# A fused Mamba-like block and FP4 feed-forward on one core: the gate and silu(z) moved within a step, h's transposes kept together, and a down product of 17 passes

## What is computed

```
x_proj, z = split(x @ W_in)                      # 512 + 512 columns
x_conv = silu(causal_conv4(x_proj) + conv_b)
ssm = x_conv @ W_xproj                           # 1 + 16 + 16 columns
delta = softplus(ssm[..., 0]);  B, C = ssm[..., 1:17], ssm[..., 17:]
h_mean = einsum("bld,bln->bdn", x_conv, delta * B) / L     # over the whole sequence
y = (einsum("bdn,bln->bld", h_mean, C) + D * x_conv) * silu(z)
x1 = layernorm(x + y @ W_out)
h = silu(q(x1) @ q(w_gate).T) * (q(x1) @ q(w_up).T)        # 704 columns
out = layernorm(x1 + q(h) @ q(w_down).T)
```

## Time and profile before

| | us |
|---|---|
| median of 3 runs (2201.85 to 2204.41) | 2202.8 |
| the profiled execution | 2204.03 |
| its span, first to last instruction | 2202.1 |
| PE busy | 1990.6 (90%) |
| DVE busy | 1756.7 (80%) |
| POOL busy | 1115.6 (51%) |
| ACT busy | 1111.5 (50%) |

### The profile page before, as it was taken

The page is one execution under the profiler, slowest core; times in us unless marked ns, Lnnn a source line. Parts: engine busy times, 40 slices in busy tenths (PEclk is TensorE's granted clock), DMA queues, the critical chain, the costliest instruction groups (busy, mean ns, idle before and its releaser), DMA issues.

```text
span 2202.1 us, 37847 instructions
## 1 busy us (share of the span) xinstructions
PE 1990.6 (90%) x10532; PEld 1583.8 (72%) x10532; DVE 1756.7 (80%) x3548; ACT 1111.5 (50%) x2100; POOL 1115.6 (51%) x1643
## 2 busy tenths in 40 slices
PE   1887899899999999899999999899999999877776
PEld 1655688688877888688877888688876888666665
DVE  6234788798978888789877888798887888788875
ACT  2665455555545555455544556455544555423332
POOL 2223455466545556455644555465554556445543
PEclk9999999999999999999999999999999999999998
DMA  2111111111111111111111111111111111000000
GB/s 79 50 56 43 34 49 44 44 43 45 49 41 34 44 48 45 36 49 49 41 38 41 44 44 48 38 49 44 39 41 39 49 45 35 29 20 25 20 20 15
DMA packets 77089, 90.53 MB, mean 41 GB/s; under 512 B 8881, under 2 KB 59953, under 8 KB 76849
## 3 DMA queue, kind: packets, MB, share of 16 engines
q1 hardware_dynamic: 76848, 87.73, 12.2%
HBM read 37.37 MB, written 16.78 MB: 25 GB/s over the span
## 4 chain that ended last, share of the span: by engine, by line
PE 76%; issue 5%; DVE 4%; ACT 3%; POOL 1%; ACTq 0%; DVEq 0%; POOLq 0%
PE pgu L489 23%; PE pd L489 14%; PE pd L537 9%; PE pa L489 6%; PE pb L489 6%; PE pc L571 4%; PE pc L519 4%; PE pe_ L631 2%; PE pa L559 2%; PE pc L496 2%; PE pe_ L548 1%; PE pd L638 1%; DVE hbuf L990 1%; DVE qsh L820 1%; PE pa L615 1%
## 5 line engine op out<-in xcount | busy, mean ns | idle before, releaser
L489 PE MATMUL pgu<-wgu_hi,xqT 128*128 128x512 f32 (+1 forms) x1536 | 427.7, 387 | 0.9 <-issue 0.9
L489 PE MATMUL pd<-wd_hi,hqT 128*128 128x256 f32 (+1 forms) x1536 | 334.5, 299 | 18.7 <-DVE r L1012 15.5
L489 PEld LDWEIGHTS pgu<-wgu_hi,xqT 128*128 128x128 f32 x1536 | 279.8, 190 | 75.8 <-issue 27.6
L537 PE MATMUL pd<-wout,g 128*128 128x256 f32 x1024 | 259.9, 398 | 49.6 <-DVE hqT L980 35.2
L489 PEld LDWEIGHTS pd<-wd_hi,hqT 128*128 128x128 f32 (+1 forms) x1536 | 255.8, 190 | 57.4 <-issue 23.8
L946 DVE SCALAR_TENSOR_TENSOR acc<-xps,cw,acc 128x512 f32<-128x512 f32 x256 | 248.7, 972 | 24.4 <-POOL acc L429 23.7
L418 POOL TENSOR_SCALAR rs<-mv 128x1 f32<-128x1 f32 x128 | 61.6, 481 | 396.4 <-DVE mv L1027 228.8
L537 PEld LDWEIGHTS pd<-wout,g 128*128 128x128 f32 x1024 | 191.5, 195 | 79.7 <-issue 56.0
L741 ACT ACTIVATE hqT<-pe_ 128x512 fp32r<-128x512 f32 x128 | 76.2, 595 | 335.3 <-PE pe_ L631 335.3
L402 POOL TENSOR_TENSOR xv<-xnq,qsx 128x256 f32<-128x256 bf16 x128 | 79.5, 621 | 300.1 <-DVE xnq L839 300.1
L489 PE MATMUL pgu<-wgu_lo,xqT 128*128 128x512 f32 (+1 forms) x768 | 228.3, 379 | 0.0
(11 more groups left out here) (132 smaller groups left out, 4669.2 us busy)
## 6 DMA issues: line engine op xcount, KB each, us to landing
xcr<-xcs SPq DMA_DIRECT2D x128, 256.0 KB, 2.3
xin<-in_L_attn_x_dram SPq DMA_DIRECT2D x32, 512.0 KB, 3.9
xres<-in_L_attn_x_dram SPq DMA_DIRECT2D x128, 128.0 KB, 2.1
out_dram<-outb SPq DMA_DIRECT2D x128, 128.0 KB, 1.7
szr<-in_L_attn_W_in_dram SPq DMA_DIRECT2D x1, 1024.0 KB, 7.4
szr<-in_L_ffn_w_down_dram SPq DMA_DIRECT2D x1, 704.0 KB, 8.6
szr<-in_L_ffn_w_gate_dram SPq DMA_DIRECT2D x1, 640.0 KB, 4.5
szr<-in_L_ffn_w_up_dram SPq DMA_DIRECT2D x1, 640.0 KB, 5.7
```

The lines of the kernel that those rows point to most:

```text
L489: mm = pe.matmul(bank, lhsT, rhs, start=(m == 0), stop=(m == len(pairs) - 1))
L537: mm = pe.matmul(pd[:, 0:DM], g[:, (s + 1) % 2, c, j * P:(j + 1) * P], wout[:, c, :], start=(c == 0), stop=(c == NB - 1))
```

## The change

Four edits, all in the steps and in the weights' setup.

1. The last chunk of h (64 columns) is written twice by POOL, side by side, in place of 64 columns of zeros, and the last chunk of the down weights is laid out twice: in wd_hi, rows 0 to 63 keep the high half, and rows 64 to 127 hold the low half. One pass over 128 rows then gives high x high and high x low, and one over 64 rows low x high: 17 passes in place of 18.
2. The banks pd and pe_ become one tensor pde of two banks. The six transposes of h go to its last 768 columns with one semaphore increment, and ACT and DVE each take them in one instruction. They have waited for r1 and r2 from the first transpose on.
3. POOL's gate stands behind the history copy and xprod.
4. ACT's silu(z) stands behind the first tap and the copy of the transposed x.

```diff
@@ POOL, setup
+            pool.wait_ge(wq_ready, 3)
+            for h in range(KM):
+                rest = quant_w[2][:, h * FF + FC * P:(h + 1) * FF]
+                pool.tensor_copy(twice_d[:, h * P:h * P + FR], rest)
+                last = pool.tensor_copy(twice_d[:, h * P + FR:(h + 1) * P], rest)
+            last.then_inc(wq_ready, 1)
@@ POOL, body
-                    if p2 and not late_y(j, s):
-                        gate(i, j, s, w)
                     if p1:
...
                         pool.tensor_tensor(blocks(xv[:, :]), blocks(xnq[:, :]), spread(qsx[:, 1, :]),
                                            ALU.mult).then_inc(xprod_done, 1)
+                    if p2 and not late_y(j, s):
+                        gate(i, j, s, w)
...
                         pool.wait_ge(hq_link, 6 * tg + 6)
+                        at_least(pool, hq_pe, tg)
+                        pool.tensor_tensor(blocks(hbuf[:, 2 * FF:FF + (FC + 1) * P]), blocks(hnq[:, FC * P:FF]),
+                                           spread(qsh[:, 1, FC * P // QB:QH]), ALU.mult)
                         pool.tensor_tensor(blocks(hbuf[:, FF:2 * FF]), blocks(hnq[:, :]),
                                            spread(qsh[:, 1, :]), ALU.mult).then_inc(hprod_done, 1)
@@ PE
-                for c in range(FC + 1):
-                    m_ = P if c < FC else FR
-                    pairs += [(hqT[0:m_, c, :], wd_hi[0:m_, c, :]),
-                              (hqT[0:m_, c, :], wd_lo[0:m_, c, :]),
-                              (hqT[0:m_, FC + 1 + c, :], wd_hi[0:m_, c, :])]
-                split_product(pd[:, 0:DM], DM, pairs).then_inc(dn_pe, 1)
+                for c in range(FC):
+                    pairs += [(hqT[:, c, :], wd_hi[:, c, :]),
+                              (hqT[:, c, :], wd_lo[:, c, :]),
+                              (hqT[:, FC + 1 + c, :], wd_hi[:, c, :])]
+
+                pairs += [(hqT[:, FC, :], wd_hi[:, FC, :]),
+                          (hqT[0:FR, 2 * FC + 1, :], wd_hi[0:FR, FC, :])]
+                split_product(pde[:, 0:DM], DM, pairs).then_inc(dn_pe, 1)
...
-                        for n in range(4):
-                            mm = pe.transpose(pe_[:, n * P:(n + 1) * P],
-                                              hbuf[:, FF + n * P:FF + (n + 1) * P], ident[:, :])
-                        mm.then_inc(hq_pe, 1)
-
                         at_least(pe, r_done, capped(to, NT))
                         at_least(pe, r2_done, td)
-                        for n in range(4, FC + 1):
-                            mm = pe.transpose(pd[:, (n - 4) * P:(n - 3) * P],
-                                              hbuf[:, FF + n * P:FF + (n + 1) * P], ident[:, :])
+                        for n in range(FC + 1):
+                            mm = pe.transpose(hq_cols[:, n * P:(n + 1) * P], hbuf[:, FF + n * P:FF + (n + 1) * P],
+                                              ident[:, :])
                         mm.then_inc(hq_pe, 1)
@@ ACT
-                    if not late_y(j, s) and p1:
-                        silu_z(i, j, s, u, w)
...
                         act.activation(xqT[:, 0:KM, :], pe_[:, 0:DM].rearrange("p (c n) -> p c n", c=KM), ACT.Copy)\
                             .then_inc(xqT_hi, 1)
+                    if not late_y(j, s) and p1:
+                        silu_z(i, j, s, u, w)
@@ DVE, weights
                 dve.wait_ge(wt_hi, n + 1)
+                if lo is None:
+                    dve.tensor_tensor(hi[FR:P, :], (pa, pb)[n % 2][FR:P, 0:DM], hi[FR:P, :], ALU.subtract)\
+                        .then_inc(wt_lo, 1)
+                    continue
```

More of the change, by code:

```diff
@@ L460, in weight_groups @@
                         groups.append((P, pieces, wgu_hi[:, k, lo:lo + width], wgu_lo[:, k, lo:lo + width]))
-            for c in range(FC + 1):
-                m = P if c < FC else FR
-                pieces = [(quant_w[2][:, h * FF + c * P:h * FF + c * P + m], P) for h in range(KM)]
-                groups.append((m, pieces, wd_hi[0:m, c, :], wd_lo[0:m, c, :]))
+            for c in range(FC):
+                pieces = [(quant_w[2][:, h * FF + c * P:h * FF + (c + 1) * P], P) for h in range(KM)]
+                groups.append((P, pieces, wd_hi[:, c, :], wd_lo[:, c, :]))
+            pieces = [(twice_d[:, h * P:(h + 1) * P], P) for h in range(KM)]
+            groups.append((P, pieces, wd_hi[:, FC, :], None))
             return groups
         W_GROUPS = weight_groups()
-        W_NEEDS = [1] * 4 + [2] * 4 + [3] * (FC + 1)
+        W_NEEDS = [1] * 4 + [2] * 4 + [3] * FC + [4]
         @block.tensor
@@ L1011, in body @@
                         dve.wait_ge(xres_landed[j % 2], 16 * (2 * i + j // 2 - 1))
-                        dve.tensor_tensor(r1[:, j, :], pd[:, 0:DM], xres[:, j % 2, :], ALU.add)\
+                        dve.tensor_tensor(r1[:, j, :], pde[:, 0:DM], xres[:, j % 2, :], ALU.add)\
                             .then_inc(r_done, 1)
@@ L1040, in body @@
                         at_least(dve, out_ready, td)
-                        dve.tensor_tensor(r2[:, :], pd[:, 0:DM], r1[:, (j - 3) % TPS, :], ALU.add)\
+                        dve.tensor_tensor(r2[:, :], pde[:, 0:DM], r1[:, (j - 3) % TPS, :], ALU.add)\
                             .then_inc(r2_done, 1)
```

47 lines of the change are left out of this document (21 added, 26 removed).

## The result

The changed kernel takes 2221.2 us (median of four runs, 2221.0 to 2223.4) against 2202.3 for the kernel before: 1.0087 times, with a 95% interval of 1.0069 to 1.0104. The direction is the one forecast, but the forecast was 2240 us, +37, and the loss is 18.9, half of that.

A forecast was written before the change was run, and what follows sets the result against it. PE, tied with a loop through ACT, DVE and POOL, bounds the middle; a chain bounds the tail. Middle +14.3, +4.2, +6.6, passages +3.6, tail +13.2, start -5: +37, 2240 us; range 2228 to 2253, 8 in 10 2213 to 2257.

The forecast's parts named there:

- The tail: Steps after the last input supertile, bound by a chain: +0.94 us in each of 14 with a gate, +13.2.
- the caught scale: DVE's 44-column scale of h, blocked until POOL's running gate ends: +0.90 us in the tail, partly absorbed in middle steps.
- the row: h's transposes in one 768-column row: covered in the middle, +0.16 us on the tail's x chain.
- The step from j = 2: Middle step to j = 3, bound by the h transposes' loop: +0.55 us in each of 26 steps, +14.3.
- The second write: POOL's 64-column write ahead of hprod, in the loop of the h transposes: +0.25 us, bounds 0.15 and 0.31.
- The wait for hprod: PE waits for POOL's hprod before the h transposes, which start at about 8.3 instead of 7.73: +0.55 us.
- The loop: Closed chain through ACT, DVE, POOL and PE's h transposes, tied with PE's own work, slack about 0.07 us.
- this part costs nothing: The second write is free in steps holding input transposes or partial state, where PE comes clearly after hprod.
- The pairs from j = 0: Steps j = 0 to 2, 20 pairs: +0.45 for the first step, -0.12 for the second, +6.6 us together.
- the wait for xprod: PE's stall for xprod in the step j = 0 to 1 goes away, so +0.45 us was taken there.
- j = 3 to 0: Middle step set by PE: -0.12 for the pass, +0.33 for later r1, +0.21 us in each of 20, +4.2.
- Start and the ends of phase 1: Start: taps and x operations freed from the gate and silu(z), -5 us; no change named for phase 1's last steps.

The follow-up runs named there:

- e1: Changed kernel with only POOL's gate put back at the head of the step; 2225.0 us, 1.0108 times the kernel before.
- f1: e2 with h's transposes in two parts again, leaving the 17-pass product and the second write; 2212.5 us, 1.0051 times the kernel before.
- e3: Changed kernel with the gate waiting until DVE's 44-column scale of h has ended; 2219.9 us, 1.0074 times the kernel before.
- e2: Changed kernel with both the gate and silu(z) put back at their old places; 2217.1 us, 1.0074 times the kernel before.
- f3: f1 without POOL's second write, leaving out that part of the product; 2190.6 us, 0.9945 times the kernel before.
- f2: f1 with silu(z) moved behind abs(h); 2217.3 us, 1.0060 times the kernel before.
- f4: f2 with the gate behind xprod while there are input tiles, at the step's head in the tail; 2237.2 us, 1.0149 times the kernel before.
- g1: f1 with POOL's second write behind hprod, only PE's sixth transpose waiting for it; 2208.8 us, 1.0028 times the kernel before.

## Why the forecast came out as it did

*The tail* was right in mechanism, place and size: +0.90 for the caught scale and +0.16 for the row were forecast, less the pass, and the undisturbed step is 13.63 for 13.64. e1 and f1 bear the terms out one by one: 0.89 for the scale (12.74 to 13.63), 0.15 for the row (12.59 to 12.74), 0.11 for the pass. e3 shows the scale to be the cause. What the forecast did not see is that this blocked scale hides another cost: without it the long wait of the wide row comes with half clock on PE in most of the tail's steps (e1, e2, e3), and only two parts give a tail that gains (f1). Why the changed kernel has the same wait at full clock in 12 of 14 steps stays open.

*The step from j = 2* was right in its place and 0.12 too large. Of its terms, silu(z) was put at +0.33 and measures 0.27 (e2 to e1). The second write was put at +0.25 and measures 0.18 (f3 to f1). The wait for hprod is where it was said to be, and the saved pass is lost in it. Two things were set wrongly: the caught scale was called hidden here by that wait, but it costs 0.28 by itself (f2 to f4); and the terms don't add, since they lie on one chain: 0.27, 0.18 and 0.28, less 0.12 for the pass, would be 0.61, and all together make 0.43. That the 0.55 came near is partly luck: two terms were too large and one was left out.

*The loop was named in part.* Through PE's transposes of h it closes at j = 2 only (f3). With the gate at its old place a delay of POOL also reaches r1 at j = 0 and PE's W_xproj at j = 3, by way of the DVE operation that the gate blocks (f3, g1). The forecast knew this block, from the earlier trace rows, and used it for the gain of moving the gate; it didn't use it for what the write ahead of the gate costs. That "this part costs nothing" at j = 3 is refuted for f1, where the write costs 0.23. In the changed kernel the gate no longer stands there, and j = 3 moved by 0.02.

*The pairs from j = 0* were put at +0.33 each and came to -0.14. That is the largest term that failed, 9.4 us of the 18 by which the sum was too high. There the wait for xprod goes with the freed operation on x (0.43 for 0.93), and that gain, in DVE's chain, outweighs silu(z) and the write: from e1 to the changed kernel j = 0 falls by 0.65. The forecast had taken 0.10 off for the wait for xprod.

*j = 3 to 0*: the delay of r1 was taken as a stall of 0.33 us ahead of the down product. Its working doesn't give this 0.33: 0.90 less the waits of 0.35 and 0.5 that it names leaves 0.05, and less the first alone 0.55. The stall is 0.18, about the 0.19 that the kernel before has in its step from j = 2, and the saved pass covers most of it: +0.02.

*Start and the ends of phase 1* gave 5 us more than forecast. Most of it came in two steps in which the granted clock was higher than before: the second behind the first r1, 17.74 us at 0.91 instead of 19.33 at 0.84, and the last of phase 1, 23.49 at 0.86 instead of 25.74 at 0.82. The forecast left the clock out altogether. These 5 us, the 9.4 of the pairs, the 3.7 of j = 3 and the 3.3 of j = 2 lie on the same side, so the total missed by half, though the tail came out near.

## What to carry to other kernels

When a short operation takes longer than its size, look for the engine that it shares a port with before moving anything: an instruction put ahead of a long POOL operation is also put ahead of the two-input operations of DVE that are issued during it (in f1, L851 beside the gate). Undo each part of a change and also join the parts, since costs on one chain hide each other; here the parts cost 39 and 16 us and the whole 19. Count a longer wait of TensorE at half clock behind it as well, and compare step by step with the granted clock beside it.

## What was not expected of the hardware

- The clock in the middle of steady work: the eight matmuls of 256 columns behind a wait of 2.09 us ran in 1.97 us or in 3.65 from one step to the next, at granted clocks of 1.00 and 0.88 for the step; behind 1.73 us in all 14 steps of f1's tail in 1.97.
- The order of two issues 0.04 to 0.06 us apart decided over 0.71 us of POOL's time, and with it over 0.70 us of the step within one kernel (f1: 14.39 and 15.09).
- A pass of 256 columns fewer shortened even the tail's step, in which PE is busy 9.8 of 12.6 us, by 0.11: the down product lies on the loop there.
